# Masked attention over 200 items: key and value tiles of 25,600 bytes a row in place of 12,800

## The reference

```python
scaler = jnp.float32(D) ** 0.5                        # B, L, D = 512, 200, 64
q = target_key @ W_target.T
k = jnp.einsum('bld,ed->ble', item_keys, W_item)
v = jnp.einsum('bld,ed->ble', item_values, W_value)
scores = jnp.einsum('bd,bld->bl', q, k) / scaler
scores = scores + -100000000.0 * (1.0 - mask.astype(scores.dtype))
w = jax.nn.softmax(scores, axis=1)
return jnp.einsum('bl,bld->bd', w, v)
```

## Time and profile before

| | us |
|---|---|
| median of 3 runs | 138.47 |
| the profiled execution | 138.77 |
| its span, from first to last instruction | 136.8 |
| TensorE busy with matmuls | 73.5 (54% of the span) |
| VectorE, ScalarE, GpSimd busy | 11.4, 8.3, 6.3 |
| SyncE's DMA queue (q1) | 52.43 MB, 91.8% of the 16 DMA engines' span |

### The profile page before, as it was taken

How to read it: one execution, slowest core, us unless ns; L and a number is a source line. 1 busy time by engine, 2 the same in 40 slices (tenths; PEclk the granted TensorE clock), 3 DMA queues, 4 the chain that set the end, 5 groups by cost and what they waited for, 6 DMA issues and landing times.

```text
span 136.8 us, 2915 instructions
## 1 busy us (share of the span) xinstructions
PE 73.5 (54%) x1354; PEld 50.1 (37%) x1354; DVE 11.4 (8%) x38; ACT 8.3 (6%) x26; POOL 6.3 (5%) x18
## 2 busy tenths in 40 slices
PE   0023994536856543568555543695555543696562
PEld 0002452324643322346443331274443331275441
DVE  5000101300000000400000000230000000230000
ACT  0300000300000000300000000120000000110001
POOL 7700000100000000100000000010000000010000
PEclk9999999995599999955999995559999995559999
DMA  4999999999999999999999999999999999999700
GB/s 105 411 375 395 413 416 424 423 430 431 419 423 423 413 427 423 439 428 427 427 416 423 419 428 418 433 430 428 427 419 416 423 434 416 422 449 396 283 26 10
DMA packets 5722, 53.32 MB, mean 390 GB/s; under 512 B 1232, under 2 KB 1296, under 8 KB 1616
## 3 DMA queue, kind: packets, MB, share of 16 engines
q1 hardware_dynamic: 4752, 52.43, 91.8%
q10 hardware_dynamic: 960, 0.72, 1.6%
HBM read 53.02 MB, written 0.13 MB: 388 GB/s over the span
## 4 chain that ended last, share of the span: by engine, by line
DMA 88%; PE 5%; SPq 3%; issue 1%; ACT 0%; DVE 0%
DMA value_ring<-values 88%; PE ps_context L374 2%; PE ps_context L388 2%; SPq L148 2%; SPq L157 1%; PE ps_small L397 0%; PE ps_context L382 0%; PE ps_small L407 0%; SPq L154 0%; ACT result L235 0%; DVE context L307 0%; ACT context_t L230 0%; PE ps_small L398 0%
## 5 line engine op out<-in xcount | busy, mean ns | idle before, releaser
L346 PE MATMUL ps_scores<-key_ring,sta_query 128*32 128x200 f32 x512 | 29.2, 377 | 26.1 <-DMA key_ring<-keys 25.6
L346 PEld LDWEIGHTS ps_scores<-key_ring,sta_query 128*32 128x32 f32 x512 | 16.6, 120 | 36.7 <-DMA key_ring<-keys 29.5
L374 PE MATMUL ps_context<-value_ring,sta_full 128*32 128x128 f32 x512 | 21.1, 314 | 16.4 <-DMA value_ring<-values 16.4
L374 PEld LDWEIGHTS ps_context<-value_ring,sta_full 128*32 128x32 f32 x512 | 15.5, 125 | 21.5 <-DMA value_ring<-values 20.5
L388 PE MATMUL ps_context<-value_ring,sta_half 128*32 128x128 f32 x256 | 16.3, 317 | 0.0
L388 PEld LDWEIGHTS ps_context<-value_ring,sta_half 128*32 128x32 f32 x256 | 12.1, 124 | 0.5
L382 PE MATMUL ps_context<-value_ring,sta_eighth 128*32 128x128 f32 x32 | 7.5, 325 | 0.3 <-DMA value_ring<-values 0.3
L189 POOL COPY half_twice<-expd 128x128 f32<-128x128 f32 x4 | 1.4, 349 | 112.9 <-ACT expd L218 112.9
L273 DVE TENSOR_TENSOR biased<-ps_scores,mask_bias 128x200 f32<-128x200 f32 x4 | 1.5, 366 | 54.3 <-PE ps_scores L346 54.3
L325 PE MATMUL ps_small<-w_query_sb 64*64 64x128 f32 x2 | 0.7, 444 | 8.5 <-DMA w_query_sb<-w_query 8.5
L307 DVE COPY context<-ps_context 128x128 f32<-128x128 f32 x4 | 1.2, 292 | 46.4 <-PE ps_context L388 46.4
(11 more groups left out here) (37 smaller groups left out, 27.9 us busy)
## 6 DMA issues: line engine op xcount, KB each, us to landing
key_ring<-keys SPq DMA_DIRECT2D x16, 1600.0 KB, 29.0
value_ring<-values SPq DMA_DIRECT2D x15, 1600.0 KB, 29.0
value_ring<-values SPq DMA_DIRECT2D x1, 1024.0 KB, 28.5
value_ring<-values SPq DMA_DIRECT2D x1, 576.0 KB, 29.5
mask_sb<-mask_rows ACTq DMA_DIRECT2D x1, 400.0 KB, 14.6
targets_sb<-targets ACTq DMA_DIRECT2D x1, 128.0 KB, 10.4
out<-result ACTq DMA_DIRECT2D x4, 32.0 KB, 8.3
w_query_sb<-w_query ACTq DMA_DIRECT2D x1, 32.0 KB, 7.7
```

Of the source, the lines that this page charges most:

```text
L346: last = nc.tensor.matmul(ps_scores[g * GU:(g + 1) * GU, 0:L], window(sta_query, PITCH, g, s * PAIRS_T + k), key_ring[:, s, c:c + KB], sta ...
L374: nc.tensor.matmul(ps_context[g * GU:(g + 1) * GU, 0:VB], window(sta_full, PITCH, g, s * PAIRS_T + k), value_ring[:, s, c:c + VB], start=s ...
```

## The change

NT goes from 4 to 2, so that a tile is 6400 columns (25,600 bytes a row, 3200 KB) and a block has two key tiles and two value tiles. The rings keep their size. A value tile now has two matmuls for items 192 to 199 (`EIGHTHS_T`), and their columns lie between those of the full and the half part. The last value tile comes in four pieces of 2048, 2048, 1280 and 1024 columns, each with a semaphore. `project` of the block before follows the last score group of a block instead of the second of four.

```diff
-NT = 4
+NT = 2
+EIGHTHS_T = GRP // NT
-    CUT = N_FULL * VB
+    CUTS = (N_FULL * VB // 2, N_FULL * VB, (N_FULL + EIGHTHS_T + N_HALF // 2) * VB, VCOLS)
                     if n == NBLK - 1 and s == NT - 1:
-                        sp.dma_start(value_ring[:, s, 0:CUT], tile[:, 0:CUT]).then_inc(s_value[s], 16)
-                        sp.dma_start(value_ring[:, s, CUT:], tile[:, CUT:]).then_inc(s_value_rest, 16)
+                        begin = 0
+                        for c, end in enumerate(CUTS):
+                            sp.dma_start(value_ring[:, s, begin:end], tile[:, begin:end]) \
+                                .then_inc(s_value_piece[c], 16)
+                            begin = end
             def weigh(n, s):
-                pe.wait_ge(s_value[s], 16 * (n + 1))
+                in_pieces = n == NBLK - 1 and s == NT - 1
+                if in_pieces:
+                    pe.wait_ge(s_value_piece[0], 16)
+                else:
+                    pe.wait_ge(s_value[s], 16 * (n + 1))
...
                 for k in range(PAIRS_T):
+                    if in_pieces and k == PAIRS_T // 2:
+                        pe.wait_ge(s_value_piece[1], 16)
...
-                c = (N_FULL + N_HALF) * VB
-                nc.tensor.matmul(ps_context[s * GU:(s + 1) * GU, 0:VB],
-                                 sta_eighth[:, s].rearrange("p i e -> p (i e)"), value_ring[:, s, c:c + VB],
-                                 start=False, stop=False)
+                if in_pieces:
+                    pe.wait_ge(s_value_piece[2], 16)
+                for k in range(EIGHTHS_T):
+                    c = (N_FULL + k) * VB
+                    g = s * EIGHTHS_T + k
+                    nc.tensor.matmul(ps_context[g * GU:(g + 1) * GU, 0:VB],
+                                     sta_eighth[:, g].rearrange("p i e -> p (i e)"),
+                                     value_ring[:, s, c:c + VB], start=False, stop=False)
                 for k in range(HALVES_T):
+                    if in_pieces and k == HALVES_T // 2:
+                        pe.wait_ge(s_value_piece[3], 16)
...
-                    if n > 0 and s == 1:
+                    if n > 0 and s == NT - 1:
                         project(n - 1)
```

More of the change, by code:

```diff
@@ L41, in masked_attention_kernel @@
     KCOLS = N_FULL * KB
-    VCOLS = (N_FULL + N_HALF + 1) * VB
+    VCOLS = (N_FULL + N_HALF + EIGHTHS_T) * VB
     assert FULL + HALF + EIGHTH == L and 2 * D == P and B % P == 0
-    CUT = N_FULL * VB
+    CUTS = (N_FULL * VB // 2, N_FULL * VB, (N_FULL + EIGHTHS_T + N_HALF // 2) * VB, VCOLS)
     out_blocks = out.rearrange("(n u) d -> n u d", u=P)
@@ L106, in masked_attention_kernel @@
         s_value = [sem(f"s_value{s}") for s in range(NT)]
-        s_value_rest = sem("s_value_rest")
+        s_value_piece = [sem(f"s_value_piece{c}") for c in range(len(CUTS))]
         s_key_used = sem("s_key_used")
@@ L378, in weigh @@
                     pe.wait_ge(s_sta_rest, 3 * (n + 1))
-                if n == NBLK - 1 and s == NT - 1:
-                    pe.wait_ge(s_value_rest, 16)
-                c = (N_FULL + N_HALF) * VB
-                nc.tensor.matmul(ps_context[s * GU:(s + 1) * GU, 0:VB],
-                                 sta_eighth[:, s].rearrange("p i e -> p (i e)"), value_ring[:, s, c:c + VB],
-                                 start=False, stop=False)
+                if in_pieces:
[6 more added lines that the diff above has]
+                                     value_ring[:, s, c:c + VB], start=False, stop=False)
                 for k in range(HALVES_T):
+                    if in_pieces and k == HALVES_T // 2:
+                        pe.wait_ge(s_value_piece[3], 16)
                     for g in range(GRP):
-                        c = (N_FULL + k * GRP + g) * VB
+                        c = (N_FULL + EIGHTHS_T + k * GRP + g) * VB
                         last = nc.tensor.matmul(
@@ L444 @@
     half = half.transpose(0, 2, 4, 6, 3, 1, 5, 7).reshape(tiles, P, HALVES_T * GRP * 2 * D)
-    eighth = v[..., FULL + HALF:L, :].transpose(0, 1, 2, 4, 3, 5).reshape(tiles, P, 2 * D)
+    eighth = v[..., FULL + HALF:L, :].transpose(0, 1, 2, 4, 3, 5).reshape(NBLK, NT, EIGHTHS_T, P, 2 * D)
+    eighth = eighth.transpose(0, 1, 3, 2, 4).reshape(tiles, P, EIGHTHS_T * 2 * D)
     arrays = {
@@ L452 @@
         "keys": k,
-        "values": np.concatenate([full, half, eighth], axis=2),
+        "values": np.concatenate([full, eighth, half], axis=2),
     }
```

## The result

| | before | changed |
|---|---|---|
| median of 15 runs, us | 138.69 | 137.50 |
| lowest and highest | 138.43, 139.40 | 137.01, 138.75 |
| ratio, 95% interval | | 0.992 (0.9905 to 0.9936) |
| profiled execution, its span | 138.77, 136.8 | 138.12, 135.6 |

The ratio says 1.1 us less. The runs of the changed kernel lie further apart than those before. Beside the later experiments, on another chip, it was run again: 137.91 against 138.61, ratio 0.9963 (0.994 to 0.9985). So 0.4 to 0.8% is what I would promise. The span, from the first to the last instruction, fell by 1.2 us both times: from 136.8 to 135.6 in the profiled executions here, and from 136.6 to 135.4 in the medians of the second comparison.

The account below looks back on a forecast made before the run. Bound by DMA: a never-dry queue sets the last landing, plus 4.9 us. Rows 0.90, completions 0.13 (together 1.0) and pieces 0.05 give 1.05 less: 138.77 to 137.72, median 0.30 lower, 137.4; range 136.5 to 138.9.

Parts of the forecast that it names:

- Rows: Tile transfers, per engine: 112 fewer rows at 0.008 us beyond their bytes, 0.90 us less.
- The line through two packet sizes: Packets of 4608 and 12,800 bytes: slope 0.300 us per 8192 bytes, fixed part 0.011 a row; 0.008 was taken.
- The upper bound: Split of the last tile: one transfer more cost 0.14 us, so 14 fewer give 2.0; rival D, 136.5, chance 0.13.
- The 0.13 that the sum had for 14 completions: DMA queue, per engine: 14 fewer transfer completions at 0.009 us each, 0.13 us less.
- The pieces: Last value tile in four pieces: 8 matmuls instead of 9 behind the last landing, 0.07 us less, taken as 0.05.
- Small loads: Start: small packets wait for longer rows, targets up to 4.7 us later, mask up to 8.9; late start stays hidden.
- The queue never ran dry: Transfers are issued 29 us ahead; later slot release loses 7 us of that and costs nothing.
- The clock (B): Last block: a falling clock makes TensorE late at the end, so slower, 139.4 in the middle case; chance 0.11.
- The decision point: Last block: TensorE's backlog sets the end from 2.6 us at the low clock level on.
- 7.0 and 12.8 us for 200 records: Last block after 123.1: TensorE's time for 4 x 50 matmul records at the high and the low clock level.
- the sign of B: End of the kernel: no idle on TensorE before the last piece would show that TensorE is late; chance 0.11.
- The slowest engine: End of the DMA: last engine done 2.7 us after the mean; as many instruction packets, so this lag was left unchanged.

Follow-up runs that it names:

- experiment 1: Changed kernel with each tile but the last laid out as two halves, so rows of 12,800 bytes in 19 transfers: 138.65 us, ratio 0.9993 to the kernel before.
- experiment 2: Kernel before with every tile except the last laid out as two halves, so rows of 6400 bytes in 33 transfers: 140.70 us, ratio 1.0138.
- experiment 6: Changed kernel with both key tiles, and both value tiles, of blocks 1 and 2 in one transfer of 51,200-byte rows: 137.24 us; beside its control 137.44.
- experiment 4: Changed kernel with the last value tile in two pieces (4096 and 2304 columns) instead of four: 137.91 us, ratio 0.9943 to the kernel before.
- experiment 3: Kernel before with only its last value tile cut into four pieces (1024, 1024, 640 and 512 columns): 138.36 us, ratio 0.9968.
- Experiment 7: Changed kernel with the last block's first value tile in two transfers (2048 and 4352 columns): 137.62 us; beside its control 138.01.
- experiment 5: Changed kernel with 8 of the 32 score matmuls of a key tile, output not the reference's: 136.65 us, ratio 0.9812 to the kernel before.
- the control: Changed kernel unmodified, run again on another chip beside the 51,200-byte-row and early-piece kernels: 137.91 us, ratio 0.9963 to the kernel before.
- edits 6 and 7: Changed kernel with 51,200-byte rows in blocks 1 and 2, the early value piece in the last block, and a fifth last piece, together: 137.53 us, ratio 0.9873.

## Why the prediction was right

137.4 was forecast and 137.5 measured, and the step that carried it is shown: the gain is in the number of rows. The second comparison gives 0.5 to 0.7 us of time where 1.05 was forecast, but 1.2 of span. The last landing is used at 130.78, where 130.8 was forecast.

- **Rows.** 0.008 us for each of 112 rows was the term. Experiments 1, 2 and 6 give 0.008 to 0.011 by landings, on rows of 6400 to 51,200 bytes. By times, experiment 2 gives 0.008; experiment 1 gives 0.008 against the first ratio of the changed kernel, 0.003 against the second, and 0.009 to 0.010 by the median spans (136.6 against 135.5 and 135.4). The line through two packet sizes of one trace had it right, with some luck: its own margin of 0.003 is 0.3 us on 112 rows. The trace had more rows to check it by. Two further windows before, 130.6 to 130.9 and 130.9 to 131.2, hold three 4608-byte rows each at 11.1%, which is 0.178 us a row, and with it the line gives 0.008 where the rows shown gave 0.011. The upper bound, 0.14 for a transfer, was a pair of landings with other things in it: experiment 1 has 14 transfers fewer than before and gains nothing. The 0.13 that the sum had for 14 completions no run shows by itself.
- **The pieces.** I took 0.05 for 8 matmuls instead of 9, and charged two more transfers in the sum of rows. The rows at the end give 0.18 (0.89 - 0.71) for it, so the sum there is 1.07 + 0.18 and not 1.0 + 0.05. Set against a wide tile in two pieces, the four save 0.6 us behind the last landing (experiment 4). Against the kernel before, the changed one has about as many records behind the last landing (16 and 18), so this term stays small; it is the finer end that keeps it so. In experiment 3, four pieces gained 0.4 where 0.2 was expected, with its interval from 0.3 to 0.6; in its trace the records cost as priced and the added rows don't show.
- **Small loads.** First scores near 18 and the mask used from about 25.6: measured 16.96 and 24.17. They wait longer the longer the rows are: targets took 14.2 us from issue in the changed kernel, 9.9 in experiment 1, 7.0 in experiment 2. From 12 to 24 us the changed kernel's two queues show 191 and 189 packets, so a turn is one row here. With that the Trainium skill's rule of a turn per packet ("DMA: Bandwidth & Descriptors", section "Queues, rings and completion order") agrees, though not its typical packet of 9 to 17 descriptors. The queue never ran dry, as forecast.
- **The clock (B).** It fell more often, as said, and TensorE did work from 122.98 on without a pause, 3.9 us of it at 0.50. The decision point was 2.6 us at the low level, and yet the end was on time. The sizes were off: 7.0 and 12.8 us for 200 records were scaled up from single tiles of 50. Yet short bursts cost more per record: at 1.00, 16 records take 0.64 us, 32 take 1.08 and 64 take 1.95, some 0.2 us a burst and 0.027 a record. In one run of work, 76 records take 3.86 us at 0.50 (0.051 each, not 0.064) and 64 take 1.95 at 1.00 (0.030, not 0.035). With 3.86 us and 0.46 x 3.46 = 1.6 at the low level, 107 records go there and 93 x 0.030 = 2.8 remain: 122.98 + 5.5 + 2.8 = 131.3. The prediction's sum gives 122.98 + 7.3 + 0.45 x 5.5 = 132.8, and 131.49 was measured. The 0.2 between 131.3 and 131.49 is about the 0.17 that the weights waited for the last landing. So the sign of B, no wait before the last piece, did not come, but only just. Experiment 7 took that work off the end and gained nothing. The Trainium skill's rule in "TensorE: Matmul & The Clock Gate", section "Loop structure matters more than you think", that a loop which waits for DMA lets the clock drop, holds for the clock here (0.835 in the mean against 0.875 before); the time fell all the same.
- **The slowest engine.** I left its lag as it was; it stayed (one tile 0.9 us late). In experiment 5, with three instruction packets fewer, the last landing moves by 1.3 us, more than the whole change moved it (1.07).

What stays open: single executions of the changed kernel lie between 137.0 and 138.9, wider than before. The listed spans show two parts of it. Four of the control's 12 have a span of 136.4 to 136.9 where the others have 135.3 to 135.6, and six take 0.4 to 0.6 us more outside the span. What causes either, and why edits 6 and 7 don't add, is open. Where instruction packets fall among the engines is a candidate for the first that no run here isolates.

## What to carry to other kernels

Where a kernel is bound by one full DMA queue, as this one is, count rows and not transfers: each row cost its bytes and a fixed 0.008 to 0.011 us on its engine here, which two packet sizes at the end of one trace already told. Where a change is worth less than 1%, compare the spans and the landings too, and not the times alone. Make rows longer in the middle, where a ring is freed in time, and keep the last tile in small pieces. Then look at what else stands in the engines' queues, down to the program itself.

## What the runs showed of the hardware that was not expected

- Ten packets of instructions, 0.16 MB beside 52.43 MB, seem to hold back the end: with seven the last piece landed 1.3 us earlier. TensorE's matmuls were fewer too, so the packets' part is inferred.
- The gain of longer rows does not stop at 12,800 bytes: from 25,600 to 51,200 a row is still worth 0.008 us, by the same distance in two pairs of traces.
- Long rows delay small loads on another queue, a row for each of their packets: 7.0, 9.9 and 14.2 us to the targets' landing with rows of 6400, 12,800 and 25,600 bytes.
- The time outside the span has two levels: 1.9 to 2.0 us in most executions, 2.3 to 2.6 in two of 23 of the kernel before and in six of 12 of the changed one on the same chip.
